# A causal attention stage: one ring of four PSUM banks for scores and turns, and the denominators' chain one step later

## The reference

```
q = apply_rope(x @ wq); k = apply_rope(x @ wk); v = x @ wv      # k and v repeated 4 times
scores = jnp.einsum('bhqd,bhkd->bhqk', q, k) / HEAD_DIM ** 0.5
scores = jnp.where(causal[None, None], scores, -jnp.inf)
out = jnp.einsum('bhqk,bhkd->bhqd', jax.nn.softmax(scores), v)
return out @ wo
```

## Time and profile before

| | us |
|---|---|
| median of 3 runs (3278.37 to 3286.23) | 3279.88 |
| the profiled execution's own time | 3280.95 |
| its span, first to last instruction | 3278.8 |
| PE busy | 2826.2 (86%) |
| DVE busy | 1325.4 (40%) |
| ACT busy | 860.3 (26%) |
| POOL busy | 779.9 (24%) |

### The profile page before, as it was taken

One profiled execution on the slowest core, in us unless ns is written; L12 is line 12 of the kernel. 1 busy time (PEld: TensorE's weight loads), 2 busy tenths in 40 slices (PEclk: granted clock), 3 DMA queues, 4 the chain that ended last, 5 costly groups with the idle time before them and its releaser, 6 DMA issues.

```text
span 3278.8 us, 46466 instructions
## 1 busy us (share of the span) xinstructions
PE 2826.2 (86%) x16154; PEld 2342.6 (71%) x16154; DVE 1325.4 (40%) x2276; ACT 860.3 (26%) x1573; POOL 779.9 (24%) x1110
## 2 busy tenths in 40 slices
PE   7968777773978777049999999999999999999998
PEld 6843333331756665039999999999999999999997
DVE  6745555551778888411321322322313313223211
ACT  2115444451144444111221211211212212112110
POOL 4523434441332232440110111011111101110110
PEclk9968888885988898569999999999999999999999
DMA  3125555542211221320320321212212203212110
GB/s 100 35 59 92 101 95 98 94 81 57 83 65 44 71 77 43 96 75 11 99 83 26 103 69 58 87 52 77 86 31 94 93 10 110 78 49 90 45 42 22
DMA packets 116217, 228.09 MB, mean 70 GB/s; under 512 B 33038, under 2 KB 34734, under 8 KB 115952
## 3 DMA queue, kind: packets, MB, share of 16 engines
q1 hardware_dynamic: 94272, 165.43, 19.8%
q0 software_dynamic: 21808, 60.65, 6.0%
HBM read 148.77 MB, written 38.94 MB: 57 GB/s over the span
## 4 chain that ended last, share of the span: by engine, by line
PE 55%; POOL 2%; issue 1%; DMA 0%; DVE 0%; DVEq 0%; ACT 0%; POOLq 0%
PE ex_hid L1727 28%; PE ex_acc L103 9%; PE ex_acc L102 9%; PE ex_acc L104 9%; POOL slot_table_dram L1550 2%; PE ex_xb L1697 1%; DMA ex_ys<-xn_dram,ex_rows_in 0%; POOL out_dram L1579 0%; DVE ex_ys L1640 0%; POOL ex_xg L1545 0%; POOL ex_ys L1560 0%; PE ex_acc L1697 0%; DVE ex_xT0l L1623 0%; DVEq L72 0%; ACT ex_xT0h L1590 0%
## 5 line engine op out<-in xcount | busy, mean ns | idle before, releaser
L1648 DVE SCALAR_TENSOR_TENSOR ex_h0l<-ex_hid,ex_h0h 128x640 fp32r<-128x640 f32 x128 | 105.6, 825 | 690.6 <-ACT ex_h0h L1607 690.6
L1648 DVE SCALAR_TENSOR_TENSOR ex_h1l<-ex_hid,ex_h1h 128x640 fp32r<-128x640 f32 x128 | 105.5, 824 | 613.7 <-ACT ex_h1h L1607 550.2
L596 DVE TENSOR_REDUCE at_nb<-at_sc 128x2 f32<-128x512 f32 (+1 forms) x384 | 245.7, 682 | 148.3 <-PE at_sc L659 147.1
L1607 ACT ACTIVATE ex_h0h<-ex_hid 128x640 fp32r<-128x640 f32 x128 | 90.2, 704 | 739.0 <-PE ex_hid L1727 732.5
L1607 ACT ACTIVATE ex_h1h<-ex_hid 128x640 fp32r<-128x640 f32 x128 | 90.2, 704 | 737.5 <-PE ex_hid L1727 701.1
L558 ACT ACTIVATE at_pT<-at_st 128x512 f32<-128x512 f32 x384 | 208.6, 597 | 261.7 <-PE at_st L671 260.3
L102 PE MATMUL ex_acc<-ex_w_h,ex_h1h 128*128 128x512 f32 x640 | 254.1, 397 | 0.0
L102 PE MATMUL ex_acc<-ex_w_h,ex_h0h 128*128 128x512 f32 x640 | 252.9, 395 | 0.0
L103 PE MATMUL ex_acc<-ex_w_l,ex_h0h 128*128 128x512 f32 x640 | 250.6, 392 | 0.0
L103 PE MATMUL ex_acc<-ex_w_l,ex_h1h 128*128 128x512 f32 x640 | 250.6, 392 | 0.0
L104 PE MATMUL ex_acc<-ex_w_h,ex_h1l 128*128 128x512 f32 x640 | 249.9, 390 | 0.0
(11 more groups left out here) (267 smaller groups left out, 5980.7 us busy)
## 6 DMA issues: line engine op xcount, KB each, us to landing
ex_raw<-in_w_tiles_dram SPq DMA_DIRECT2D x256, 256.0 KB
at_qs<-at_qT_hi SPq DMA_DIRECT2D x256, 64.0 KB, 2.8
x_in<-in_x_dram SPq DMA_DIRECT2D x32, 256.0 KB
at_q_in<-act SPq DMA_DIRECT2D x16, 512.0 KB
at_qs<-at_qT_lo SPq DMA_DIRECT2D x128, 64.0 KB, 2.6
act<-at_raw SPq DMA_DIRECT2D x128, 64.0 KB
at_recb<-o_rec_dram SPq DMA_DIRECT2D x32, 256.0 KB
op_x<-in_x_dram SPq DMA_DIRECT2D x32, 256.0 KB
```

The costliest lines, as they stand in the source:

```text
L596: dve.tensor_reduce(nb[e][:, r, p % 2, heads, qb], sc[n % 3][:].rearrange("p (h k) -> p h k", h=heads.stop - heads.start), AX.X, ALU.max, ...
L1607: act.activation(h[f % 2][0][:], hid[:, :, 0:HB], ACT.Relu).then_inc(sm["h_hi"], 1)
L1648: dve.scalar_tensor_tensor(h[f % 2][1][:], hid[:, :, 0:HB], 0.0, f32(h[f % 2][0][:]), ALU.max, ALU.subtract).then_inc(sm["h_lo"], 1)
```

## The change

- PSUM: the three banks `at_sc` and the bank `at_tb` become one ring of four, `at_ring`. Scores, the turned maxima m, the turned keys k and the two turns of queries q0, q1 take its banks in the written order `TURNS`; each waits for the reader of the bank four places before (`taken`).
- PE: in a piece, the transposed scores of half h - 2 (`shifted`) come first, then the products of queries and keys, and the masks are added last. The number of matmuls stays as it was. `turn_k` and `turn_q` stand before `values` of their piece.
- ACT keeps the maxima after piece 0 (was 1) and the queries after pieces 3 and 5 (was 4 and 5). DVE keeps k after piece 2 (was 3), and takes the reciprocals after piece 4 (was 1).
- The denominators have two buffers. Their reciprocals are stored at the head of SP's next step (h - 5 in place of h - 4), ahead of `load_stack`; the broadcast (h - 5 in place of h - 4) stands ahead of `o_den` and the four DMAs of `act`, where it stood behind them; POOL multiplies in the odd step after.

```diff
-        den = s.sb("at_den", [P, 32])
+        den = [s.sb(f"at_den{i}", [P, 32]) for i in range(2)]
-        sc = [s.ps(f"at_sc{i}", [P, D]) for i in range(3)]
+        ring = [s.ps(f"at_ring{i}", [P, D]) for i in range(4)]
-        tb = s.ps("at_tb", [P, 512])
+        TURNS = (("s0", "s1", "m", "s2", "s3", "s4", "s5", "k", "s6", "s7", "q0", "s8", "s9", "s10", "s11", "q1"),
+                 ("s0", "s1", "m", "s2", "s3", "s4", "s5", "k", "s6", "s7", "s8", "s9", "s10", "s11"))
...
# SP
+                if within(h - 5, 0, HALVES):
+                    wait_apart(sp, sm["den_turned"], h - 5 + 1, passed_sp)
+                    wait_apart(sp, sm["recb_loaded"], 16 * (h - 5), passed_sp)
+                    sp.dma_start(o_rec.rearrange("j (a b) -> (j a) b", b=32), rec[:]).then_inc(sm["rec_stored"], 16)
                 if within(h + 1, 0, HALVES):
                     load_stack(...)
-                if within(h - 4, 0, HALVES):
-                    (the same store, for h - 4)
                 if within(h - 1, 0, HALVES):
                     (two DMAs of maxima)
+                if within(h - 5, 0, HALVES):
+                    b, part = j - 3 + e, slice(64 * (1 - e), 64 * (1 - e) + 64)
+                    wait_apart(sp, sm["rec_stored"], 16 * (h - 5) + 16, passed_sp)
+                    wait_apart(sp, sm["attn_done"], b, passed_sp)
+                    sp.dma_start(recb[part, :, :].rearrange("p u n -> p (u n)"),
+                                 o_rec.unsqueeze(1).to_broadcast([UN, HD, TPB * D])).then_inc(sm["recb_loaded"], 16)
                 if within(h - 3, 0, HALVES):
                     (o_den and the four DMAs to act)
-                if within(h - 4, 0, HALVES):
-                    (the same broadcast, for h - 4)
                 if within(h - 3, 0, HALVES):
                     wait_apart(sp, raw_moved[i], 80 * b + 80, passed_sp)
-                    sp.dma_start(den[:], ...)
+                    sp.dma_start(den[i][:], ...)
...
# DVE
-                    if p == 1 and within(h - 4, 0, HALVES):
+                    if p == 4 and within(h - 4, 0, HALVES):
...
# PE
                 for p in range(6):
-                    if live_s:
-                        given = score(h, i_s, p)
                     if live_d:
                         shifted(h - 2, i_d, p)
                     if live_s:
-                        score_heads(h, i_s, p, *given)
+                        score(j, q, e, p)
```

More of the change, by code:

```diff
@@ L565, in step @@
                         keep_sums(h - 2, 0, e, j - 1)
-                    if e == 0 and p >= 4 and within(j + 1, 0, B):
-                        q_hi(j + 1, p - 4, [(q_loaded[(2 * q + k) % 4], 192 * w + 192) for k in range(2)])
+                    if e == 0 and p in (3, 5) and within(j + 1, 0, B):
+                        q_hi(j + 1, p // 4, bank(q, e, f"q{p // 4}"), [(q_loaded[(2 * q + k) % 4], 192 * w + 192) for k in range(2)])
             steps(act, first, step)
@@ L611, in _, with taken, turn_q @@
         def _(pe):
-            def turn_q(b, rd):
+            def taken(j, q, e, name):
+                h, at = 2 * j + e, TURNS[e].index(name)
+                last, back = (TURNS[e][at - 4], 0) if at >= 4 else (TURNS[1 - e][at - 4], 1)
+                h = h - back
+                if last[0] == "s" and within(h, 0, HALVES):
+                    pe.wait_ge(sm["maxima"], ONE + PIECES * h + int(last[1:]) + 1)
+                if last == "m" and within(h - 1, 0, HALVES):
+                    pe.wait_ge(sm["m_kept"], ONE + h)
+                if last == "k" and within(h + 1, 0, HALVES):
+                    pe.wait_ge(sm["k_kept"], ONE + h + 2)
+                if last[0] == "q" and within(j + 1, 0, B):
+                    pe.wait_ge(sm["q_lo"], ONE + 2 * j + 2 + int(last[1:]) + 1)
+                return bank(q, e, name)
+            def turn_q(j, q, rd):
+                x = taken(j, q, 0, f"q{rd}")
                 if rd == 0:
[L614 to L617, removed]
+                    pe.wait_ge(sm["q_in_loaded"], ONE + 16 * (j + 1) + 16)
                 for a in range(2):
@@ L642, in turn_m, with score @@
                     .then_inc(sm["m_turned"], 1)
-            def score(h, i, p):
+            def score(j, q, e, p):
+                i = 2 * q + e
                 width = P if p < 2 else S
                 heads = range(REP) if p < 2 else range(p // 2 * 2 - 2, p // 2 * 2)
[L647 to L653, removed]
@@ L655, in score_heads @@
-            def score_heads(h, i, p, heads, width, banks):
+                banks = [taken(j, q, e, f"s{2 * p + r}")[:].rearrange("p (h k) -> p h k", k=width) for r in range(2)]
                 for c, n in enumerate(heads):
@@ L658, in score_heads @@
                         rows = slice(64 * r, 64 * r + 48)
[L659 to L663, removed]
+                        pe.matmul(banks[r][:, c, :], qs[i][rows, p % 2, n, width - P:width],
+                                  ks[i][rows, p % 2, 0:width], start=True, stop=False, skip_group_check=True)
+                for r in range(2):
+                    pe.matmul(banks[r][:, :, width - P:width], t["identb"][:],
+                              t["mask"][:].unsqueeze(1).to_broadcast([P, len(heads), P]), start=False, stop=True,
+                              skip_group_check=True).then_inc(sm["scores"], 1)
             def shifted(h, i, p):
@@ L690, in first @@
                 for rd in range(2):
-                    turn_q(0, rd)
-                turn_k(0, 0, 0)
+                    turn_q(-1, 1, rd)
+                pe.wait_ge(sm["q_lo"], ONE + 2)
+                turn_k(-1, 1, 1)
             def step(j, w, q, e):
```

92 lines of the change are left out of this document (41 added, 51 removed).

## The result

The changed kernel takes 3351.9 us (median of 4 runs, 3342.7 to 3354.6), the kernel before 3280.4 us beside it: ratio 1.021, 95% interval [1.0186, 1.0235], slower by 71 us. The forecast was 3323 us, +43 us. The profiled execution took 3354.6 us, with a span of 3352.4 us.

The account below looks back on a forecast made before the run. SP's queue, 32.1 us a pair of steps, was taken as the bound. 3280.95 + 45 (26 steps x 1.72) - 1.5 = 3324.5 us profiled, 3323 us median; range 3272 to 3357, likeliest case 3299 to 3357.

Parts of the forecast that it names:

- SP's queue is the floor: In attention, SP's queue needs 32.1 us a pair of steps, which nothing on PE, DVE or ACT can lower.
- PE's own 30.0 us a pair: PE's pair of steps in steps 2 to 4, before reciprocals were on DVE's path; 2.1 us below SP's floor.
- rival C: SP is not the bound and the stall's end counts: pairs fall towards PE's 30.0 us, 3230 us; chance 0.11.
- Ring and order cost 0: PE's new order, ring and earlier copies: up to 2.1 us a pair either way is hidden under SP.
- The reciprocals' stall goes: DVE's stall of about 6 us in the even step goes; by itself at most 1.75 us a pair gained.
- The broadcast ahead of the sums: In SP's queue the sums land only behind the broadcast: 1.7 to 3.9 us more a step.
- I take 2.6: nearer the lone broadcast: Added us a step for sums behind the broadcast, chosen near its 5.8 alone, half a microsecond for stack and maxima.
- The head store costs nothing: The store heading SP's step finds reciprocals done; the broadcast's wait for it is covered by 7.6 us of stack DMAs.
- The tail: After step 30 the chain from denominators to product sets the pace: 0 us, from -3 to +4.
- this wait hidden: The broadcast's wait for POOL's product, early in the odd step, is hidden since SP trails PE.
- B: Rival: the sums pass the broadcast in the DMA engines, so no change, 3275 us; chance 0.13.
- D: Rival: the DMA queue is worse, sums landing 10.0 us after the broadcast's issue, +105, 3383 us; chance 0.10.

Follow-up runs that it names:

- e1: The changed kernel with the broadcast again behind o_den and the four DMAs of sums: 3358.7 us, ratio 1.0233.
- e2: The kernel before with only the broadcast moved ahead of o_den and the four DMAs of sums: 3322.1 us, ratio 1.0124.
- e4: The changed kernel with o_den ahead of the broadcast on its own semaphore, for which alone the load of denominators waits: 3311.6 us, ratio 1.0096.
- e6: The changed kernel with the store of reciprocals behind the stack again and two buffers for the reciprocals: 3352.4 us, ratio 1.0215.
- e11: The changed kernel with the broadcast written to the other 64 partitions than the sums, each half's rows getting the other's reciprocals: 3311.1 us, ratio 1.0106.
- e3: The changed kernel with the broadcast as four DMAs of 16 partitions each, in the same place: 3302.4 us, ratio 1.0058.
- e9: The kernel of e8 with the queries' load issued one step earlier, ahead of the odd step's broadcast: 3241.2 us, ratio 0.9889.
- e10: The kernel of e9 with the two DMAs of the turned maxima issued by ACT in place of SP: 3221.7 us, ratio 0.9827.
- e5: The changed kernel with the whole denominator chain put back as before, leaving ring, PE's order and earlier copies: 3278.6 us, ratio 0.9991.
- e12: The kernel before with only the queries' load a step earlier and the maxima's two DMAs issued by ACT: 3267.1 us, ratio 0.9958.
- e7: The changed kernel with SP's order of before, the chain still a step later, two buffers for the reciprocals: 3274.0 us, ratio 0.9975.
- e8: The kernel of e7 with o_den on its own semaphore, for which alone the load of denominators waits: 3272.2 us, ratio 0.9972.

## Why the prediction was right, and what it mis-sized

**SP's queue is the floor: right.** e1, e2, e4, e6 and e11 change only what SP's queue waits for and how long (e3 adds three issues), and the time follows. Without any wait a step of SP is 16.05 - 0.83 = 15.22 us; this and the measured waits (e3: and 1.1 us of issues) give each step of e1 to e4, e6, e11 and the changed kernel within 0.3 us: for the changed kernel 15.22 + 4.47 = 19.69, measured 19.88. The floor of 32.1 us a pair held 1.66 us of waits for sums; without them e9 ran at 31.0. PE's own 30.0 us a pair was near as well: e10 has 29.4, and its 3222 us lie by the 3230 of rival C, which needed SP out of the way.

**Ring and order cost 0: right under SP's cover** (e5). Where SP was not yet the bound, in steps 0 to 3, they gained 7.3 us, which I had not counted (7.2 in e5, whose median keeps 3.6 of them). With the queue relieved, ring, order, the later reciprocals and e4's semaphore are together worth 45 us (e12 against e10), the first three by themselves at least some 25. They were not tried apart there.

**The reciprocals' stall goes, and SP does not gain by it: right.** DVE's 56.7 us of waits for the denominators are gone after, and the step is longer all the same.

**The broadcast ahead of the sums: the cause was right, its size was not.** The step that was mis-sized is "I take 2.6: nearer the lone broadcast". It makes 5.07 + 2.6 = 7.67 us from broadcast to load; the trace has 8.74. The 26 steps cost 76.4 us in place of 45, 31 us more, where the profiled execution (3354.6) lies 30 us above 3324.5. That the two agree is luck: the 7.3 us won in the first steps and the 6.2 us lost at the end, neither of them in the forecast, nearly cancel. The 2.6 was also more than its own parts give: 5.8 alone, 1.0 for the sums and 0.5 for what is just ahead are 7.3 us from broadcast to load, so 2.2. This 7.3 is what e2 and e11 measure (7.31, 7.25). I read the traffic behind the broadcast as the one thing that slows it. e11 shows what I had left out: broadcast and sums write the same 64 partitions in the changed kernel, and that costs 1.5 us a step and 41 us in all. In other halves the term is 7.25 us, and the time 3311. So it is in part luck that 8.74 us and 3352 us lie in the stated range: its upper end, 9.0 us and 3357 us, was there for stack and query loads behind the broadcast, and these do not follow it here.

The Trainium skill ("SBUF — State Buffer", "Door 1: The DMA port swizzle") has partitions 0 to 63 on eight of the memory's DMA ports and 64 to 127 on the other eight. By that page the two transfers of the changed kernel share eight ports. e11 agrees in its sign and gives the 1.5 us; no run here shows a port.

**The head store costs nothing: right here, but the reason was incomplete.** I had looked only at what it waits for from DVE. It also waits for the last broadcast, which the wait for the sums already covered. Each of the two moves is enough by itself to put the broadcast's landing into SP's step: e1 (store alone) 20.20 us, e6 (broadcast alone) 19.89, the change 19.88, neither (e7) 16.74. That is why undoing one brings nothing.

**The tail: forecast 0, -3 to +4; measured +6.2.** Most of it is one event, of after, in the timelines of SP and POOL:

```profile
808.16 0.33 SPq L456 DMA_DIRECT2D o_rec_dram<-at_rec  x1
814.39 0.59 SPq L469 DMA_DIRECT2D at_recb<-o_rec_dram  x1
...
811.94 2.35 POOL L522 TENSOR_TENSOR act<-act,at_recb 128x1024 f32<-128x1024 f32 x1
```

The broadcast waits for POOL's product, which ends at 814.29; by the next step's distance from store to broadcast (823.47 to 825.02) it could have gone at 809.7. I had called this wait hidden. It is read from the trace and was not tried.

**The rivals.** B is refuted: the sums did not all pass the broadcast (8.74 us from broadcast to load, where B needs about 0.8 + 5.07 = 5.9). D is refuted, 8.7 us against its 10.0, though its direction was right. C is refuted for the change as made. Beside e4, the expectations of e7 and e8 failed since a third loop lay close by, the load of queries behind the broadcast; e9 shows it.

## What to carry to other kernels

Before a transfer is moved in a queue, list every wait that its landing ends, also on the semaphore that guards its buffer's next use: if one of them comes less than its landing time later in the same queue, the queue stands for the rest of the landing. A broadcast with few rows outermost is a slow transfer that others stand behind; cut it so that each part covers 16 partitions, or place it where nothing is asked of the queue's next ones. And a floor in the issuing queue hides what a compute change is worth: relieve the queue (an issue moved to an idle engine, a load moved a step ahead), then judge the change; here ring and order were worth 0 us under the queue's cover (e5), and with the later reciprocals between some 25 and 45 us without it (e12).

## What the runs showed of the hardware

The 256 KB broadcast in one DMA held up the 64 KB transfers behind it, by the load that waits for them until 8.7 us after its issue, when they wrote the same 64 partitions, and 7.3 us when they wrote the other 64. In four DMAs of 16 partitions, SP's wait for the transfers behind it was 1.65 us in place of 4.47, and 148 small packets were counted in place of 88. The Trainium skill ("DMA: Bandwidth & Descriptors", "Rules for kernel authors") says that an outermost dimension of size c, below 16, keeps a DMA to at most c engines. The one broadcast has 4 rows outermost, each of the four has 16 partitions; e3 agrees, by its small packets. The issue of a DMA of 64 KB from tile to tile held SP's queue for about 0.6 us (4 in 2.60 us at 403.03), that of a store or load of 16 KB for 0.3 to 0.55 us, and that of each quarter of the broadcast for 0.43 us (4 in 1.73 us, e3). Taking two issues a step away from a queue that was the bound shortened the step by 0.82 us (15.51 to 14.69), until SP waited for the queries' halves again.
